# Stacking keys and queries in three transfers instead of twelve, with the masked keys on every fourth partition

## What is computed

```
x  = x + attention(layernorm(x), context)
x  = x + ffn(layernorm(x))

attention(q, k):
    qh = q @ Wq.T     # 32 heads of 16
    kh = k @ Wk.T     # 8 groups of 16, each for 4 heads
    vh = k @ Wv.T
    attn = softmax(qh @ kh / 4)
    out  = (attn @ vh) @ Wfc.T + bfc
```

## Time and profile before

| | |
|---|---|
| median of 3 runs | 450.9 us (450.56 to 450.95) |
| profiled execution | 450.88 us |
| its span | 448.9 us |
| mean granted TensorE clock | 0.981 |
| PE busy | 421.3 us (94%) |
| DVE, ACT, POOL busy | 331.0, 314.4, 238.3 us |
| all transfers | 49.79 MB |

### The profile page before, as it was taken

How to read it: one execution, slowest core, us unless ns; L and a number is a source line. 1 busy time by engine, 2 the same in 40 slices (tenths; PEclk the granted TensorE clock), 3 DMA queues, 4 the chain that set the end, 5 groups by cost and what they waited for, 6 DMA issues and landing times.

```text
span 448.9 us, 11824 instructions
## 1 busy us (share of the span) xinstructions
PE 421.3 (94%) x4620; PEld 343.5 (77%) x4620; DVE 331.0 (74%) x711; ACT 314.4 (70%) x578; POOL 238.3 (53%) x226
## 2 busy tenths in 40 slices
PE   6876969899999999999999999999999999899987
PEld 6745848766887889878887889778887889558973
DVE  3787477976997679975997689966997589466432
ACT  7748794888479756987479756977489745994441
POOL 5578991698328823685328814684338712690000
PEclk9969798999999999999999999999999999999999
DMA  7888669364801551034601552035502251000001
GB/s 273 311 229 316 222 177 287 115 218 113 213 4 43 149 139 53 1 96 139 144 4 45 163 116 60 9 92 153 130 3 57 66 124 45 1 25 26 2 26 47
DMA packets 21239, 49.79 MB, mean 111 GB/s; under 512 B 4672, under 2 KB 5184, under 8 KB 21184
## 3 DMA queue, kind: packets, MB, share of 16 engines
q1 hardware_dynamic: 20862, 48.24, 37.5%
q10 hardware_dynamic: 322, 0.80, 0.7%
HBM read 23.86 MB, written 4.19 MB: 62 GB/s over the span
## 4 chain that ended last, share of the span: by engine, by line
PE 71%; POOL 9%; ACT 6%; DVE 5%; issue 5%; DMA 1%; ACTq 1%; POOLq 0%; DVEq 0%
PE bank L659 23%; PE bank L679 10%; POOL plo L1350 7%; PE bank L452 6%; PE bank L533 6%; PE bank L453 6%; PE bank L454 6%; PE bank L566 5%; PE bank L487 3%; PE bank L584 2%; PE bank L586 2%; DVE mneg L1112 1%; DMA qs<-cq 1%; ACT phi L867 1%; ACT p L864 1%
## 5 line engine op out<-in xcount | busy, mean ns | idle before, releaser
L1350 POOL TENSOR_TENSOR plo<-p,phi 128x512 f16<-128x512 f32 x128 | 150.8, 1191 | 56.0 <-ACT phi L867 55.1
L659 PEld LDWEIGHTS bank<-x2T,wgate 128*128 128x128 fp8e4 x2048 | 117.2, 99 | 12.4 <-issue 9.8
L659 PE MATMUL bank<-x2T,wgate 128*128 128x128 fp8e4 x2048 | 126.1, 221 | 0.5 <-ACT x2T L879 0.3
L864 ACT ACTIVATE p<-bank 128x512 f32<-128x512 f32 x128 | 77.5, 606 | 17.7 <-PE bank L566 16.9
L1112 DVE TENSOR_REDUCE mneg<-bank 128x4 fp32r<-128x512 f32 x128 | 83.4, 685 | 7.1 <-PE bank L533 7.1
L867 ACT ACTIVATE phi<-bank 128x512 f16<-128x512 f32 x128 | 77.3, 604 | 0.0
L679 PE MATMUL bank<-wlin,act 128*128 128x512 fp8e4 x256 | 72.0, 378 | 0.0
L890 ACT CAST ff<-bank 128x512 bf16<-128x512 f32 x64 | 37.5, 586 | 43.3 <-PE bank L659 43.2
L886 ACT ACTIVATE gate<-bank 128x512 bf16<-128x512 f32 x64 | 38.2, 597 | 41.2 <-PE bank L659 41.0
L566 PE MATMUL bank<-qs,ks 98*128 98x512 f32 x128 | 55.3, 432 | 5.5 <-ACT phi L867 2.6
L533 PE MATMUL bank<-kmask,cq 128*128 128x512 f32 x128 | 50.9, 457 | 0.9 <-ACT cq L846 0.7
(11 more groups left out here) (117 smaller groups left out, 806.5 us busy)
## 6 DMA issues: line engine op xcount, KB each, us to landing
qs<-cq SPq DMA_DIRECT2D x90, 128.0 KB, 2.5
stage<-in_w SPq DMA_DIRECT2D x14, 512.0 KB, 5.3
ks<-khl SPq DMA_DIRECT2D x96, 64.0 KB, 2.0
cin<-in_ctx SPq DMA_DIRECT2D x8, 512.0 KB, 4.2
xr<-in_x SPq DMA_DIRECT2D x16, 256.0 KB, 4.3
out<-xr SPq DMA_DIRECT2D x16, 256.0 KB, 2.5
xr<-in_w SPq DMA_DIRECT2D x6, 512.0 KB, 6.2
raw_g<-in_w SPq DMA_DIRECT2D x4, 512.0 KB, 6.3
```

The lines of the kernel that those rows point to most:

```text
L659: mm = pe.matmul(out[:, h * SEQ:(h + 1) * SEQ], wgate8[:, UH * v + h, kk, part, :], x2T[:, b % NB, kk, :], start=kk == 0, stop=kk == KT - 1)
L864: act.activation(p32[:, e % P32BUF, :], T[n % 2][:, :], ACT.Exp, scale=QUARTER).then_inc(p32_ok, 1)
L1350: pool.tensor_tensor(plo[:, e % PBUF, :], p32[:, e % P32BUF, :], phi[:, e % PBUF, :], ALU.subtract).then_inc(plo_ok, 1)
```

## The change

The columns of Wk and Wq are put in another order on the host. Pair hp now lies on the partitions hp, hp + 4, hp + 8, ... (every fourth one). The 128 partitions of `khl`, taken in order, are then the rows of one slot of `ks`, four to a row, so that one transfer with a source of 128 partitions and a destination of 32 fills a slot: 3 transfers of 256 KB for keys in place of 12 of 64 KB, and 3 of 512 KB for queries in place of 12 of 128 KB. The bytes are the same. `mask_k` keeps its 4 transfers, with rows of a stride of four.

The four query semaphores become one, which is waited for with the keys ahead of tile 0. In the start SP issues all three transfers of queries, ACT's six are gone, and `mask_first` writes the four slabs of `kmask` whole, each as the keys times a column of `lane`, which is 1 on every fourth partition. DVE makes `lane` in one more reduction; POOL's clearing of `kmask` is gone.

```diff
             def mask_k(q):
...
-                    rows = slice(32 * hp, 32 * hp + 32)
+                    rows = slice(hp, P, PAIRS)
...
+            def stack_k(q):
+                sp.wait_ge(k_lo, 2 * (q + 1))
+                if q >= 2:
+                    sp.wait_ge(st_done, TILES * (q - 1))
                 for slot, part in enumerate((0, 0, 1)):
-                    sp.dma_start(ks[32 * slot:32 * slot + 32, q % 2, hp, :, :].bitcast(F32),
-                                 khl[32 * hp:32 * hp + 32, part, :, :].bitcast(F32)).then_inc(k_stacked, 16)
+                    sp.dma_start(ks[32 * slot:32 * slot + 32, q % 2, :, :, :].bitcast(F32),
+                                 khl[:, part, :, :].bitcast(F32)).then_inc(k_stacked, 16)
...
+            def stack_q(q):
+                sp.wait_ge(q_lo, 2 * (q + 1))
...
                 for slot, part in enumerate((0, 1, 0)):
-                    sp.dma_start(qs[32 * slot:32 * slot + 32, hp, :, :].bitcast(F32),
-                                 cq[32 * hp:32 * hp + 32, part, :, :].bitcast(F32)).then_inc(q_stacked[hp], 16)
+                    sp.dma_start(qs[32 * slot:32 * slot + 32, :, :, :].bitcast(F32),
+                                 cq[:, part, :, :].bitcast(F32)).then_inc(q_stacked, 16)
...
                 if n == 0:
-                    pe.wait_ge(k_stacked, 16 * 3 * PAIRS * (p + 1))
+                    pe.wait_ge(k_stacked, 16 * 3 * (p + 1))
+                    pe.wait_ge(q_stacked, 16 * 3 * (p + 1))
...
-                if i == 0 and g % 2 == 0:
-                    pe.wait_ge(q_stacked[g // 2], 16 * 3 * (p + 1))
...
             def mask_first():
...
                 for hp in range(PAIRS):
-                    rows = slice(32 * hp, 32 * hp + 32)
-                    ins = act.copy(kmask[rows, hp, :, :], khl[rows, 0, :, :].bitcast(F32))
+                    ins = act.activation(kmask[:, hp, :, :], khl[:, 0, :, :].bitcast(F32), ACT.Identity, scale=lane[:, hp:hp + 1])
...
-            stack_first(0)
             max_rows(0, 0)
             stack_max_first(0)
-            stack_first(1)
...
+            dve.tensor_reduce(lane[:, :], ident[:, :].rearrange("p (d h) -> p h d", h=PAIRS),
+                              AX_X, ALU.add).then_inc(lane_ok, 1)
...
-            pool.memset(kmask[:, :, :, :].bitcast(F32), 0.0).then_inc(zeroed, 1)
...
-    wk = host("L0_xattn_Wk").T.reshape(KT, P, P).transpose(1, 0, 2)
+    wk = host("L0_xattn_Wk").T.reshape(KT, P, PAIRS, 2 * HD).transpose(1, 0, 3, 2)
...
-    wq = host("L0_xattn_Wq").reshape(GROUPS, HPG, HD, KT, P).transpose(4, 3, 1, 0, 2)
+    wq = host("L0_xattn_Wq").reshape(PAIRS, 2, HPG, HD, KT, P).transpose(5, 4, 2, 1, 3, 0)
```

More of the change, by code:

```diff
@@ L13 @@
 AX_X = mybir.AxisListType.X
-AX_XY = mybir.AxisListType.XY
 P = 128
@@ L164, in xattn_ffn_kernel @@
         parity = sb("parity", [P, 2], F32)
+        lane = sb("lane", [P, PAIRS], F32)
         spare = sb("spare", [P, 1], F32)
@@ L218, in xattn_ffn_kernel @@
         k_masked, k_stacked, k_masked_first = sem("k_masked"), sem("k_stacked"), sem("k_masked_first")
-        q_stacked = [sem(f"q_stacked{h}") for h in range(PAIRS)]
+        q_stacked = sem("q_stacked")
         m_stacked = [sem(f"m_stacked{i}") for i in range(NB)]
         stored = [sem(f"stored{r}") for r in range(RING)]
-        parity_ok, filled, consts, sel_in, zeroed, ident8_ok = (
-            sem("parity_ok"), sem("filled"), sem("consts"), sem("sel_in"), sem("zeroed"), sem("ident8_ok"))
+        parity_ok, lane_ok, filled, consts, sel_in, ident8_ok = (
+            sem("parity_ok"), sem("lane_ok"), sem("filled"), sem("consts"), sem("sel_in"), sem("ident8_ok"))
         w_hi, w_clamp, w_cast, w_conv = sem("w_hi"), sem("w_clamp"), sem("w_cast"), sem("w_conv")
@@ L352, in mask_k @@
                 for hp in range(PAIRS):
-                    rows = slice(32 * hp, 32 * hp + 32)
+                    rows = slice(hp, P, PAIRS)
                     sp.dma_start(kmask[rows, hp, :, :].bitcast(F32), khl[rows, 0, :, :].bitcast(F32)).then_inc(k_masked, 16)
[L356 to L360, removed]
-                for slot, part in enumerate((0, 0, 1)):
-                    sp.dma_start(ks[32 * slot:32 * slot + 32, q % 2, hp, :, :].bitcast(F32),
-                                 khl[32 * hp:32 * hp + 32, part, :, :].bitcast(F32)).then_inc(k_stacked, 16)
[L365 to L373, removed]
+            def stack_k(q):
+                sp.wait_ge(k_lo, 2 * (q + 1))
+                if q >= 2:
+                    sp.wait_ge(st_done, TILES * (q - 1))
+                for slot, part in enumerate((0, 0, 1)):
+                    sp.dma_start(ks[32 * slot:32 * slot + 32, q % 2, :, :, :].bitcast(F32),
+                                 khl[:, part, :, :].bitcast(F32)).then_inc(k_stacked, 16)
+            def stack_q(q):
+                sp.wait_ge(q_lo, 2 * (q + 1))
+                if q:
+                    sp.wait_ge(st_done, TILES * q)
+                else:
+                    for c in range(W_KV, W_FC):
+                        sp.wait_ge(*chunk_free(c))
                     sp.wait_ge(wk_lo, 1)
                 for slot, part in enumerate((0, 1, 0)):
-                    sp.dma_start(qs[32 * slot:32 * slot + 32, hp, :, :].bitcast(F32),
-                                 cq[32 * hp:32 * hp + 32, part, :, :].bitcast(F32)).then_inc(q_stacked[hp], 16)
+                    sp.dma_start(qs[32 * slot:32 * slot + 32, :, :, :].bitcast(F32),
+                                 cq[:, part, :, :].bitcast(F32)).then_inc(q_stacked, 16)
             def stack_max(q, i):
@@ L400, in _ @@
                 load_chunk(c)
[L401 to L404, removed]
+            stack_k(0)
+            stack_q(0)
             for c in range(W_GATE + W_AHEAD, W_FREE):
@@ L421, in _ @@
                             load_chunk(c)
-                    for hp in range(PAIRS):
-                        stack_k(q, hp)
+                    stack_k(q)
                     if q + 1 < NP:
@@ L432, in _ @@
                 if q < NP:
-                    for hp in range(PAIRS):
-                        stack_q(q, hp)
+                    stack_q(q)
                 for b in downs[1:]:
@@ L816, in keys_hi @@
                 if q:
-                    act.wait_ge(k_stacked, 16 * 3 * PAIRS * q)
+                    act.wait_ge(k_stacked, 16 * 3 * q)
                 if q >= 2:
@@ L842, in queries_hi @@
                 if q and h == 0:
-                    for hp in range(PAIRS):
-                        act.wait_ge(q_stacked[hp], 16 * 3 * q)
+                    act.wait_ge(q_stacked, 16 * 3 * q)
                 act.wait_ge(q_done, 2 * q + h + 1)
@@ L907, in mask_first @@
             def mask_first():
-                act.wait_ge(zeroed, 1)
+                act.wait_ge(lane_ok, 1)
                 act.wait_ge(k_hi, 2)
                 for hp in range(PAIRS):
-                    rows = slice(32 * hp, 32 * hp + 32)
-                    ins = act.copy(kmask[rows, hp, :, :], khl[rows, 0, :, :].bitcast(F32))
+                    ins = act.activation(kmask[:, hp, :, :], khl[:, 0, :, :].bitcast(F32), ACT.Identity, scale=lane[:, hp:hp + 1])
                 ins.then_inc(k_masked_first, 1)
@@ L920, in stack_max_first @@
                               mrow[0:n, 0, :].bitcast(F32)).then_inc(m_stacked[0], 16)
[L922 to L931, removed]
             half = KT * P
@@ L1194, in _ @@
             dve.wait_ge(consts, 1)
-            dve.tensor_reduce(parity[:, :], ident[:, :].rearrange("p (k a d) -> p a k d", k=PAIRS, a=2),
-                              AX_XY, ALU.add).then_inc(parity_ok, 1)
+            dve.tensor_reduce(parity[:, :], ident[:, :].rearrange("p (a d) -> p a d", a=2),
+                              AX_X, ALU.add).then_inc(parity_ok, 1)
+            dve.tensor_reduce(lane[:, :], ident[:, :].rearrange("p (d h) -> p h d", h=PAIRS),
+                              AX_X, ALU.add).then_inc(lane_ok, 1)
             for h in range(2):
```

## The result

The changed kernel takes 470.88 us (median of 4 runs, 467.31 to 472.69) against 450.79 us. The measured ratio is 1.0406 of before, 95% interval 1.0367 to 1.0446 (the quotient of the two medians, 1.0446, is at its upper end). The forecast was no measurable change, 451.2 us in 447.8 to 452.8. The profiled execution took 467.31 us, with a span of 465.5 us where before had 448.9: 16.6 us to account for. It is the fastest of the four; the others lost 3 to 5 us more, which this trace can't show.

A forecast was written before the change was run, and what follows sets the result against it. PE's own work was taken to bound the kernel from stage 2 on, leaving only the start: tile 2's +0.4 and the clock's +0.4, half given back, made +0.4 on 450.88, 451.3, stated as 451.2 us, range 447.8 to 452.8.

The forecast's parts named there:

- I take 224 because the destination, and one queue, are as in that row: Stage 0's queries: the three transfers move 224 GB/s, as the old ones at full share, so the last land at 31.7.
- The row of 262 GB/s: Profile row at the start, read as two queues both holding queries, moving 262 GB/s at a share of 1.00.
- The slower rival: Start: weights, maxima and queries share the engines, 190 GB/s, tile 0 at about 33; 452.5 us, chance 0.20.
- SP's weights* behind the queries: Start: weights issued 3.7 us earlier, same order behind the same bytes; nothing waited for them near 38.
- Whatever the three transfers do there, within ten us it is hidden: Steady stages: queries land about ten us before the first matmul reading them, so a steady stage gains nothing.
- a steady stage longer than 50 us: Sign in the steady stages: if seen, the prediction is wrong at its root, since PE should be busy throughout.
- The wait moved to tile 0: Start: tile 0 waits for all queries, 31.7 for 29.33; tile 2 follows 3.6 later at 35.3, +0.4 us.
- The clock's halving: PE's clock after the start: +0.4 us, then half the delay given back from 44 to 50, +0.8 becoming +0.4.
- that rival: Issues with four times the rows take four times as long, so none are saved; 452.0 us, chance 0.05.
- POOL's clearing: Start: the removed 1.90 us of clearing is worth 0, as POOL then idled 3.06 us anyway.
- DVE's reduction: Start: a second reduction of some 0.3 us costs 0, as DVE idled 3.02 us ahead of 5.97.
- the mask: Start: four activations on all partitions replace four copies on 32 that took 2.51 us; taken as 0.

The follow-up runs named there:

- e5: The changed kernel with stage 0's maxima issued by SP ahead of the five weight chunks, ACT issuing no transfer: 1.0347 of before.
- e6: The changed kernel with slots on every third partition and stage 0's maxima issued by SP ahead of the weights: 1.0029 of before.
- e2: The changed kernel with only the slots of keys and queries moved to every third partition, still three transfers: 1.0079 of before.
- e3: The changed kernel with twelve transfers for the queries of stage 0 alone, all other keys and queries keeping three: 1.0182 of before.
- e10: The changed kernel itself, run again in a later batch: 1.0387 of before.
- e4: The kernel before with only the mask's part of the change, columns and transfers as before: 0.9992 of before.
- e1: The changed kernel with twelve transfers again for keys and for queries, from every fourth partition to 32 neighbouring ones, all issued by SP: 1.0098 of before.
- e9: The changed kernel with slots on every third partition, queries in twelve transfers with four semaphores, ACT issuing pair 0 and SP pairs 1 to 3 at the start: 0.9936 of before.

## Why the prediction was wrong

**"I take 224 because the destination, and one queue, are as in that row; the bounds are 425 (all as in a load) and 224 with the doubt below": this step failed.** It measured 119. With it the prediction's own sum gives 37.9 for the queries' landing and not 31.7, and 37.9 is where the trace has it. The form had no row, and I bounded it on one side only: 224 was both the value taken and the slow end. The nearest row differed in the 128 partitions of the source, four of whose rows go to one row of the slot; the lower bound should have been well under it. The row of 262 GB/s was misread as well: from 24 to 26 SP's last keys were still in flight beside ACT's queries. The slower rival had the mechanism ("all three transfers are wanted at once") but priced it from 190 GB/s, and gave it 0.20.

**"*SP's weights* behind the queries are issued 3.7 us earlier, but in the same order behind the same bytes": failed too.** They were in the same order on SP, but the maxima are on ACT's queue, issued at 25.83. Before, that was amid SP's queries and 2.4 us ahead of the first weights (28.29); now it is behind the first weights (24.84). The trace has 3.2 us from the queries' landing to tile 0; e5 gives 2.4 us of tile 0 for it, e6 against e2 3.1 us. I had looked at what the weights move past on SP's queue alone. The two steps together are the 9.4 us by which tile 0 (41.11) missed its 31.7: 6.2 by the rate and 3.2 by the maxima.

**"Whatever the three transfers do there, within ten us it is hidden": right for waits on transfers, wrong for the stage.** From the first issue to the last landing the queries of a steady stage need 15.2 us in place of 9.5 to 11.0, and still are not waited for: the last landed at 238.1, and the first matmul that reads them ran at 244.2. But PE idled for 1.19 and 2.15 us without a releaser in the change, alike (0.9 to 1.2 and 2.2 us) in e3, e5 and e10, and in no trace of the other kernels. In all four, the two idlings end 1.2 to 1.6 us after the two instruction packets that were the latest of all, by 8 and 9 us. In the other kernels no packet up to 380 us was late by more than 4.3 us. The step that failed is that transfers matter to PE only where it waits for their data: by this timing, full engines held back its instructions too. It is read from the traces; no run moved the instructions' transfers alone. The prediction had named the sign itself, a steady stage longer than 50 us, as one that makes it wrong at its root. The idling (3.3 us) and the half clock behind the second one (0.57 and 0.58 from 290 to 294) account for some 5 of the 5.5 us that the lag grew.

**The wait moved to tile 0** cost what was forecast, once the landing is put right: from tile 0 to tile 2 it took 3.5 us in the change and 3.6 in e5, as in the prediction, at half clock. **The clock's halving did not last**: the lag was 9.8 us at tile 2 (44.62 against 34.86). It shrank to 8.4 by tile 12 (61.30 against 52.86), with a shorter second stretch at half clock (a mean of 0.79 from 52 to 60, where before had 0.50 from 44 to 50). So 1.4 us were given back, not half. The third stretch was longer (0.58 from 74 to 82, where before had 0.72 from 66 to 72), and the lag was 10.4 again at stage 1's up part. In the end nothing was given back.

**Right were** the issues (three in 2.0 us, so that rival falls), POOL's clearing, DVE's reduction and the mask (e4), and ACT's six issues.

Neither of the two rules of the Trainium skill that were set against each other gives the change's rate. "SBUF — State Buffer" (Door 1: The DMA port swizzle) gives 8 of 16 ports at 27.2 GB/s to 32 neighbouring partitions, an estimate of 218 GB/s; to such a destination the runs show 118, 165 and 224, by the pattern of the source. "DMA: Bandwidth & Descriptors" (Rules for kernel authors) has small transfers coalesced; here, with slots on neighbouring partitions, 128 KB beat 512 KB (e1 1.0098, the change 1.0387). An account that fits the change can be put together from these pages of the Trainium skill (the second's section The descriptor swizzle, and the ports of the first): if engines are dealt out by the source's partition, then four source rows of an engine go to one row of the slot, and at any time the sixteen engines write to rows of 4 of the 16 ports only; at 27.2 GB/s a port this is an estimate of 109 GB/s, where 117 to 123 were measured. It also has the rate rise when the slot is spread. It is argued, not shown, and it was not tried whether it gives the 165 of e1.

## What to carry to other kernels

A transfer between SBUF partitions has a rate that depends on both partition patterns: full engines moved 117 to 123 GB/s in the change and 262 to 303 in e9's start, at the same bytes. So fewer and larger transfers are worth nothing unless their form keeps the rate. Read share and GB/s together, don't take a rate at a low share for what full engines would move, and treat a form that the trace does not have as unknown downwards too. Engines that are full can hold back more than data: here also the instructions of PE. Where the order of rows is free (here the contraction's), try source and destination both spread. And before moving an issue earlier, look for the transfer on another queue that it now passes.

## What the runs showed that was not expected

Copies from SBUF to SBUF of 32 rows moved 211 GB/s at a share of 0.94 between neighbouring partitions, 164 at 1.01 with only the source on every fourth, 205 at 0.91 with only the destination on every third, and 215 at 0.56 with both spread; e9's start, with both spread, had 303 at 1.03. A small transfer on ACT's queue landed behind large ones that SP had issued a microsecond earlier, though it is on a queue of its own: 16 KB issued at 25.83 were waited for until 41.1. And full DMA engines were joined by standstills of PE of 0.9 to 1.2 and of 2.2 us that no semaphore explains, at the same places in four traces, each ending just behind an instruction packet that came 8 or 9 us late.
